# A Mamba layer and a mixture of experts on one core: GpSimd's additions of the logarithm and its products u placed ahead of the second power

## What is computed

```python
xn = rmsnorm(layernorm(x)) ;  xs, res = split(xn @ W_in, 2)        # 512 channels each
xs = silu(causal_conv4(xs) + conv_b)
dt, Bm, Cm = split(xs @ W_x, [512, 528])                           # B and C: 16 states
dt = softplus(dt @ W_dt)
h[t] = exp(A * dt[t]) * h[t-1] + dt[t] * xs[t] * Bm[t]             # per channel and state
y[t] = sum over the 16 states of h[t] * Cm[t]
x1 = x + layernorm(ln(x) + (y * silu(res)) @ W_out)
```

## Time and profile before

| | |
|---|---|
| median of 3 runs (lowest to highest) | 2204.61 us (2198.73 to 2207.08) |
| the profiled execution's own time, and its span | 2197.51 us, 2195.8 us |
| mean granted TensorE clock | 0.844 |
| busy: TensorE / VectorE / ScalarE / GpSimd | 73% / 84% / 64% / 86% |
| the costliest group, VectorE's scans, 1024 x 1265 ns | 1243.5 us |
| GpSimd's products of states, 256 x 4814 ns | 1228.9 us |

### The profile page before, as it was taken

How to read it: one execution, slowest core, us unless ns; L and a number is a source line. 1 busy time by engine, 2 the same in 40 slices (tenths; PEclk the granted TensorE clock), 3 DMA queues, 4 the chain that set the end, 5 groups by cost and what they waited for, 6 DMA issues and landing times. The chain is left out here.

```text
span 2195.8 us, 22816 instructions
## 1 busy us (share of the span) xinstructions
PE 1604.0 (73%) x5492; PEld 632.6 (29%) x5492; DVE 1846.1 (84%) x2054; ACT 1412.9 (64%) x2547; POOL 1884.4 (86%) x786
## 2 busy tenths in 40 slices
PE   7776878696878778686878786968788784452690
PEld 3222323232322223232323232323223230111690
DVE  2478998999999989899999989999989899996312
ACT  2576777767686868686777777676868685541121
POOL 0286999999999999999999999999999999960456
PEclk9898979798898979798989797989889796665795
DMA  2673466665666675857575756656666758327752
GB/s 91 167 182 78 107 143 137 145 153 127 154 140 140 142 157 111 179 111 162 114 155 124 149 131 144 153 131 152 139 138 141 148 115 175 77 75 241 243 126 62
DMA packets 168980, 305.14 MB, mean 139 GB/s; under 512 B 27648, under 2 KB 87810, under 8 KB 168864
## 3 DMA queue, kind: packets, MB, share of 16 engines
q1 hardware_dynamic: 137696, 240.13, 44.3%
q0 software_dynamic: 30784, 62.85, 15.9%
q10 hardware_dynamic: 384, 1.05, 0.2%
HBM read 77.82 MB, written 39.52 MB: 53 GB/s over the span
## 5 line engine op out<-in xcount | busy, mean ns | idle before, releaser
L1021 DVE TENSOR_TENSOR_SCAN room<-pa,carry,room 128x512 f32<-128x512 f32 x1024 | 1243.5, 1265 | 87.9 <-ACT pa L870 55.3
L1220 POOL TENSOR_TENSOR room<-room 128x2048 f32<-128x2048 f32 x256 | 1228.9, 4814 | 54.0 <-ACT carry L863 54.0
L870 ACT ACTIVATE pa<-room,neg_a 128x512 f32<-128x512 f32 x1024 | 694.7, 687 | 370.5 <-DVE room L1021 333.6
L518 PE MATMUL py<-room,blk 128*32 128x512 f32 x2048 | 333.1, 724 | 239.4 <-POOL room L1220 132.9
L1007 DVE TENSOR_TENSOR room<-room,pb 128x2048 f32<-128x2048 f32 x176 | 398.5, 2264 | 33.3 <-DMA room<-du 33.3
L1213 POOL TENSOR_TENSOR room<-room,b_rep 128x2048 f32<-128x2048 f32 x80 | 369.0, 4612 | 36.2 <-DVE room L1021 34.8
L582 PE MATMUL pp<-xs,w_dtx 128*128 128x512 f32 x512 | 246.5, 621 | 18.9 <-DVE du L950 11.6
L546 PE MATMUL pp<-xsp,w_conv 128*128 128x512 f32 x512 | 245.3, 613 | 8.5 <-ACT xsp L736 8.4
L538 PE MATMUL pp<-xnt,w_in 128*128 128x512 f32 x256 | 177.5, 831 | 99.8 <-ACT xs L743 88.3
L518 PEld LDWEIGHTS py<-room,blk 128*32 128x32 f32 x2048 | 44.7, 117 | 439.3 <-POOL room L1220 241.8
L1186 POOL TENSOR_TENSOR du<-du,xs 128x512 f32<-128x512 f32 x64 | 93.3, 1682 | 73.6 <-DVE du L959 73.6
(11 more groups left out here) (185 smaller groups left out, 1896.5 us busy)
## 6 DMA issues: line engine op xcount, KB each, us to landing
room<-du SPq DMA_DIRECT2D x1016, 128.0 KB, 2.4
du<-du POOLq DMA_DIRECT2D x56, 512.0 KB, 6.7
room<-in_L_ffn_w_dram SPq DMA_DIRECT2D x39, 512.0 KB, 7.2
room<-bc_scratch SPq DMA_DIRECT2D x64, 256.0 KB, 5.1
du<-late POOLq DMA_DIRECT2D x28, 512.0 KB, 6.1
combine_scratch<-zeros SPq DMA_DIRECT2D x16, 520.0 KB, 9.8
xt<-in_L_attn_x_dram SPq DMA_DIRECT2D x16, 512.0 KB, 4.3
b_rep<-bc_scratch SPq DMA_DIRECT2D x64, 128.0 KB, 3.9
```

The lines of the kernel that those rows point to most:

```text
L518: mm = pe.matmul(py[32 * j:32 * j + 32, :], blk[:], h[:, quad % 4, j, :], start=(g == 0), stop=(g == 3), tile_position=(0, 32 * j))
L870: act.activation(pa[:, decay_bank(t), :], rep[:, c % 2, t % 4, 0, :], ACT.Exp, scale=neg_a[:, a_column(t):a_column(t) + 1]).then_inc(s_exp, 1)
L1021: v.tensor_tensor_scan(h[:, quad % 4, t % 4, :], pa[:, decay_bank(t), :], bq[:, quad % 2, t % 4, :], carry[:, par, t:t + 1], ALU.mult, ALU ...
L1220: pool.tensor_tensor(h[:, quad % 4], h[:, quad % 4], c_rep[:, par, quad % 4, :].unsqueeze(1).broadcast_to((P, 4, T)), ALU.mult).then_inc(s ...
```

## The change

Three entries of `PREP`'s table of slots and one of `POST`'s are other numbers:

```diff
-    ln=44, ..., add_ln=(46, 47), u=(50, 51, 60, 61),
-    rep=(53, 63, 79, 95))
+    ln=44, ..., add_ln=(44, 44), u=(48, 48, 60, 61),
+    rep=(50, 63, 79, 95))
 POST = dict(
-    ..., stats=(24, 42), pow=(27, 45), ...
+    ..., stats=(24, 42), pow=(27, 49), ...
```

More of the change, by code:

```diff
@@ L53 @@
     pe_res=(27, 30, 33, 36), act_res=(29, 32, 35, 38), silu_g=84, keep_r=24,
-    ln=44, rest=((36, 37), (52, 53)), add_e=(30, 42), add_rest=(38, 54), add_ln=(46, 47), u=(50, 51, 60, 61),
-    rep=(53, 63, 79, 95))
+    ln=44, rest=((36, 37), (52, 53)), add_e=(30, 42), add_rest=(38, 54), add_ln=(44, 44), u=(48, 48, 60, 61),
+    rep=(50, 63, 79, 95))
 FIRST = dict(
@@ L78 @@
 POST = dict(
-    load=-13, pe_out=(10, 11, 12, 13, 16, 17, 19, 20), dve_z=(15, 22), stats=(24, 42), pow=(27, 45), z2=30, x1=32,
+    load=-13, pe_out=(10, 11, 12, 13, 16, 17, 19, 20), dve_z=(15, 22), stats=(24, 42), pow=(27, 49), z2=30, x1=32,
     store_x1=35, hid=57, store_hid=59, pe_ht=(60, 63), act_ht=(62, 65), pe_w1=(66, 67), raw=70, silu=84, pe_w2=87,
```

## The result

The changed kernel takes 2187.16 us (2185.82 to 2190.24, four runs), beside 2202.86 us for the kernel before: ratio 0.9931, 95% interval 0.9908 to 0.9954. That is 15.7 us less. The forecast was 20 us less, 2184.6 us, in a range from 2172 to 2203. The profiled execution has a span of 2185.3 us.

What follows compares the result with a forecast made beforehand. A loop through GpSimd's u, the copies of block 0 and VectorE's inputs and scans sets the period. 13 x 1.5 + 0.5 = 20 us less gives 2184.6 us, range 2172 to 2203; xo's load was costed at 0.

Steps and rivals of the forecast that it cites:

- The covers: Slack before GpSimd's additions, u and ScalarE's `hid` would wait for their inputs: 2.7, 0.9, 1.0 and 5 us; cost taken: nothing.
- the thin one of 0.9 us: Second addition on GpSimd: add_e of pair 1 lands at 1127.3, the addition is sent at 1128.2 at the earliest.
- The term that was too small: GpSimd's additions and u pass the power and its product: 1.5 us per tile, bounds 1.27 and 2.16 us.
- 1.5 us or a little more: Earlier landing of the copies of block 0, with 2 more getting through ahead of add_rest; 1.5 us was taken.
- more is passed on: Rival: u moves 2.16 us or all copies precede add_rest, so VectorE's whole wait goes; 28 to 32 us, 2175 us; chance 0.12.
- it just fits; cost 0, at worst a few tenths: SyncE's queue: with xo ahead, `b_rep` lands near 1157.4, GpSimd asks at 1157.25, VectorE's scan 63 comes at 1157.3.
- the service time of 1.7 us: Time xo's load takes of all 16 DMA engines ahead of `b_rep`, from three such moves at 38.3% of 13 us.
- slower: Rival: xo holds the queue 5.6 us, `b_rep` lands 4.1 us later, GpSimd's quad 1 waits; 22 us more, 2227 us; chance 0.08.
- eaten on the way: Rival: late `b_rep` at quad 1, late add_e or unmoved copy landings leave 0 to 10 us gain, 2199 us; chance 0.20.
- the sign: A GpSimd wait for `b_rep` at L1213 would show the gain eaten on the way or a slower kernel.
- the forecast's own case: Whole kernel: gain of 14 to 26 us, chance 0.60.

Runs made afterwards that it cites:

- the third run: The changed kernel with the second power between the additions and the product of states, so ahead of u, and xo's load ahead as before: 2195.87 us.
- the second run: The kernel before with only the load of xo moved behind the copies of block 0: 2213.61 us, ratio 1.0052.

## Why the prediction was right, and where it was not

**The direction and the mechanism** were right: the loop through GpSimd's u, the copies of block 0 and VectorE's scans sets the period. GpSimd's new order made the copies 1.6 us earlier (forecast 1.5), of which the third run gives 0.36 to the additions (forecast 0.24) and 1.26 to the power (forecast 1.27). VectorE's wait fell to 0.9 us (forecast 1.0), but that agreement is in part luck: with this order alone it is 0.6. The covers were there: no wait at the additions for the logarithm or for add_e of pair 1, the thin one of 0.9 us included, none at `hid`.

**The term that was too small** is what GpSimd's order gives. The sum had 1.5 us per tile, 20 us; alone it measured 27.2 us, 116.48 - 114.32 = 2.16 us per tile. Of these, 1.6 are the earlier start of the copies. 0.3 more are their faster landing: VectorE's inputs start 32.35 us after add_e of pair 1 in a typical tile before and 30.45 with this order alone, 1.9 earlier. This is the "1.5 us or a little more" that I did not put in the sum. The working had two more copies go out ahead of add_rest; it was four, twelve of the sixteen instead of eight, since add_rest itself goes out 0.5 us later after add_e of pair 1 than before. The rest, some 0.3 us, are shorter waits behind the edge: GpSimd's wait at quad 3 fell from 0.80 us to 0.29 in the same place, where the working kept it at 0.8. The rival "more is passed on" had the size of this half, 2.16 us per tile, by luck: neither of its conditions came true. The copies moved by 1.6 us and not by 2.16, and four of them still stood behind add_rest.

**The term that was wrong** is the load: "it just fits; cost 0, at worst a few tenths" measured 11.5 us on the kernel before and 12.3 on the changed one. The working went wrong in two steps. The first is the service time of 1.7 us, taken from a stretch where the queue had 38.3% of the engines and used where it had 98.9% and more. Off the edge the load pushes the landing of `b_rep` back by 2.1 us (33.8 to 36.0 us after add_e of pair 1), and this is enough to miss the need at 35.4 by 0.6 us, which is what these tiles lose. At the edge it is 3.5 us (3.1 when the changed kernel ran again). The median time of `b_rep` to landing in the steady part is 3.9 us with the load ahead of the copies, and with the load between them and `b_rep` it is 5.3:

```profile
DMA to landing us min/median/max: 3.9/5.3/6.7
```

Its latest, 6.7 us, is 2.8 above the 3.9. The rival "slower" had the right place and needed 5.6 us; the truth lies between. Off the edge it is the rival "eaten on the way", whose condition was a `b_rep` half a microsecond late at quad 1. The prediction had named a wait of GpSimd for `b_rep` as the sign of these two rivals, and the sign stands in every tile, although the time came out in the forecast's own case. The second step is that I followed one tile, and it was of the kind without the branch. Waits for issue as long as the 2.56 us stand, in the changed kernel's steady part, only in the other kind. In the kernel before the kinds differ by a few tenths, so one tile seemed to stand for all.

So the two errors, 7 us too few in one term and 12 too many in the other, nearly cancelled. That the sum of 20 us came so close to 15.7 is luck. The Trainium skill's sentence (DMA: Bandwidth & Descriptors, on queues, rings and completion order) that each engine takes a queue's descriptors in ring order agrees with these landings: `b_rep` did not pass the load (in the tile of the queue above the load landed at 1150.6 and the parts of `b_rep` from 1152.1 on). One tile of the second run is an exception: a part of `b_rep` landed there 0.7 us ahead of the load. I had set it beside the rival and left its price at the low value.

## What to carry to other kernels

Undo each half of a change alone, also when its sum looks right: here the best kernel was half of the change, and the other half was a loss of 12 us hidden in a net gain of 16. Where DMA engines are full, cost an inserted transfer by the landing times of what stands behind it in the queue, not by the engines' time for its bytes. And in a loop over pairs of tiles read both kinds of tile: a transfer beside the loop's branch can cost what it does not cost anywhere else.

## What the runs showed that was not expected

The same 512 KB load in the same slot cost 0.4 to 0.7 us in each tile that runs straight on and 1.7 to 1.9 us in each tile with the loop's branch. At the branch VectorE stood for up to 2.6 us and ScalarE for up to 4.9 us with "issue" as the only reason, while the instruction queue had five packets instead of one among data at 98.9% of the engines. And one accumulating DMA of 512 KB left the median landing of sixteen plain copies beside it at 2.4 us, but raised the longest from 2.4 to 6.2 us.
